# Spreading decay exponents by DMA instead of rebuilding them with small matmuls, in a gated delta-rule layer stack

## The reference, cut to what matters

```python
q, k, v = (silu(causal_conv(x @ W.T)) ...)        # 16 heads, dk 64, dv 128
q, k = l2_norm(q), l2_norm(k)
alpha = exp(-exp(A_log) * softplus(x @ Wa.T + dt_bias))
beta = 2 * sigmoid(x @ Wb.T)
# per head and token:
S = a_t * (S - b_t * k_t (k_t S)) + k_t v_t
o_t = S^T q_t
out = rms_norm(o) @ Wo.T
```

## Time and profile before

| | |
|---|---|
| median of 3 runs | 1748.54 us (1748.18 to 1759.42) |
| the profiled execution | 1763.2 us, span 1761.4 us |
| mean granted PE clock | 0.943 |
| PE busy | 1635.7 us, 93% |
| DVE busy | 1209.7 us, 69% |
| ACT busy | 800.0 us, 45% |
| POOL busy | 494.5 us, 28% |
| loop over the 32 units | about 93 to 1040 us of the span |

### The profile page before, as it was taken

The page is one execution under the profiler, slowest core; times in us unless marked ns, Lnnn a source line. Parts: engine busy times, 40 slices in busy tenths (PEclk is TensorE's granted clock), DMA queues, the critical chain, the costliest instruction groups (busy, mean ns, idle before and its releaser), DMA issues.

```text
span 1761.4 us, 32553 instructions
## 1 busy us (share of the span) xinstructions
PE 1635.7 (93%) x12575; PEld 993.5 (56%) x12575; DVE 1209.7 (69%) x2261; ACT 800.0 (45%) x1403; POOL 494.5 (28%) x986
## 2 busy tenths in 40 slices
PE   5798999999999999999999998887999899899998
PEld 1124666666666756666766766434545455554555
DVE  5955887888897878886767675647556755754533
ACT  5745565675655666564554443232232233222221
POOL 1033636445454543645445360000000000000000
PEclk9886997999997999999999997898999999999999
DMA  3000000000000000000000140000000000000000
GB/s 110 1 13 12 10 17 9 10 17 10 17 9 9 18 10 17 9 18 9 18 15 12 41 152 1 1 1 1 1 1 1 7 1 1 7 1 1 7 1 7
DMA packets 61337, 26.39 MB, mean 15 GB/s; under 512 B 54000, under 2 KB 57904, under 8 KB 60800
## 3 DMA queue, kind: packets, MB, share of 16 engines
q1 hardware_dynamic: 61184, 24.32, 5.3%
HBM read 16.37 MB, written 7.34 MB: 13 GB/s over the span
## 4 chain that ended last, share of the span: by engine, by line
PE 73%; DVE 17%; ACT 6%; issue 4%; DMA 0%; SPq 0%; POOL 0%; DVEq 0%; ACTq 0%
PE bank L825 7%; PE bank L516 6%; PE bank L809 6%; PE bank L812 6%; PE bank L555 4%; PE bank L617 3%; PE bank L544 3%; PE bank L489 3%; PE bank L457 3%; PE bank L772 2%; PE bank L566 2%; PE bank L470 2%; PE bank L644 2%; DVE vc L1244 2%; PE bank L426 2%
## 5 line engine op out<-in xcount | busy, mean ns | idle before, releaser
L1323 DVE TENSOR_TENSOR AM<-bank,et 128x512 f32<-128x512 f32 x192 | 129.6, 687 | 152.5 <-PE bank L516 78.3
L1702 POOL TENSOR_TENSOR SU<-SU 128x28 f32<-128x28 f32 (+6 forms) x448 | 206.8, 462 | 35.2
L1706 POOL TENSOR_TENSOR SU<-SU 128x28 f32<-128x28 f32 (+6 forms) x448 | 203.4, 454 | 35.1
L1681 POOL TENSOR_TENSOR st<-st,nh 128x4 f32<-128x4 f32 x16 | 18.8, 1176 | 654.3 <-DVE st L1221 633.5
L1018 ACT ACTIVATE et<-bank 128x512 f32<-128x512 f32 x192 | 115.4, 601 | 189.7 <-PE bank L492 105.8
L1244 DVE SCALAR_TENSOR_TENSOR vc<-vy,conv,vc 128x512 f32<-128x512 f32 x192 | 146.4, 763 | 6.9 <-ACT vc L966 2.4
L825 PEld LDWEIGHTS bank<-WQ,AM 128*128 128x128 f32 x1024 | 129.1, 192 | 32.4 <-issue 25.0
L825 PE MATMUL bank<-WQ,AM 128*128 128x128 f32 x1024 | 138.0, 278 | 3.6 <-DVE X L1577 3.6
L809 PE MATMUL bank<-xnT,KQ 128*128 128x512 f32 x256 | 137.5, 620 | 0.0
L812 PE MATMUL bank<-xnT,KQ 128*128 128x512 f32 x256 | 133.5, 603 | 2.1 <-DVE AM L1567 2.1
L516 PE MATMUL bank<-KQ 64*128 64x256 f32 (+1 forms) x512 | 121.5, 577 | 7.7 <-DVE AM L1323 3.8
(11 more groups left out here) (223 smaller groups left out, 3441.4 us busy)
## 6 DMA issues: line engine op xcount, KB each, us to landing
scratch<-AM SPq DMA_DIRECT2D x128, 48.0 KB, 1.8
SM<-SM SPq DMA_DIRECT2D x288, 2.0 KB
SU<-scratch SPq DMA_DIRECT2D x128, 32.0 KB
WQ<-in_wqkv_dram SPq DMA_DIRECT2D x1, 2048.0 KB, 8.9
KQ<-in_wg_dram SPq DMA_DIRECT2D x4, 512.0 KB, 7.5
KQ<-in_wu_dram SPq DMA_DIRECT2D x4, 512.0 KB, 8.1
WQ<-in_wd_dram SPq DMA_DIRECT2D x1, 2048.0 KB, 15.5
WQ<-in_wo_dram SPq DMA_DIRECT2D x1, 1024.0 KB, 9.7
```

Source lines behind the costliest of these rows:

```text
L1323: e.tensor_tensor(dst, bank[(3, 1)[hh]][:, :].rearrange("p (k t) -> p k t", k=2), et[:, q % 2, :].rearrange("p (k t) -> p k t", k=2), ALU. ...
L1702: e.tensor_tensor(tmp[:, :, 0:k, 0:15 - k], sub[:, :, 0:k, k:k + 1].to_broadcast([128, 2, k, 15 - k]), sub[:, :, k:k + 1, k + 1:16].to_bro ...
L1706: e.tensor_tensor(sub[:, :, 0:k, k + 1:16], sub[:, :, 0:k, k + 1:16], tmp[:, :, 0:k, 0:15 - k], ALU.subtract).then_inc(s_su, 1)
```

## The change

The exponents are no longer rebuilt on PE. For each pair of sequences, two DMAs write the target parts of gn to a DRAM tensor, ahead. For each unit, six DMAs spread them from there over all 128 partitions into EX (one row of 512 numbers read for each partition; the last two in pieces of 128 numbers). POOL adds the causal mask in EX, in place, by six operations. The source part becomes a number per partition: four small PE transposes per pair put it into CS (`sources`), and ACT's exponential takes it as its bias, from EX; for i = 4, 5 in two halves of 256 columns, since the source block differs. The gram products go over banks 3, 1 and 2 in turn and wait for fewer `am`. The bf16 split is gone. `exp` 0 and 1 of the next unit stand late in ACT's step, ahead of `vtanh(2g)`. Some DVE calls stand in another order, and gB, gE, gD have other partitions.

```diff
-            def rows(n):
-                for k in range(3):
-                    for r in range(3):
-                        if k == 0:
-                            e.dma_start(CRt[r:r + 1, sl, :, :], spl[hs[0], r, :]).then_inc(s_rows[sl], 16)
-                        else:
...
+            def lengths(p):
+                e.wait_ge(s_gs, p + 1)
+                for k in range(2):
+                    e.dma_start(ahead[p, :, :, k, :], gn[32 * k + 32:32 * k + 48, :].rearrange("h (b t) -> h b t", b=2)).then_inc(s_row, 16)
+                e.wait_ge(s_row, 32 * p + 32)
+            def spread(n, i):
+                p, h = n // NG, GH * (n % NG) + i % 2
+                if n:
+                    e.wait_ge(s_exp, 6 * (n - 1) + i + 1)
+                if i < 4:
+                    e.dma_start(EX[:, i, :], ahead[p, h:h + 1, i // 2, :, :].rearrange("o k t -> o (k t)").to_broadcast([128, 512])).then_inc(s_ring[i // 4], 16)
+                else:
+                    e.dma_start(EX[:, i, :].rearrange("p (x t) -> p x t", x=4),
+                                ahead[p, h:h + 1, :, :, 128:256].rearrange("o b k t -> o (b k) t").to_broadcast([128, 4, 128])).then_inc(s_ring[i // 4], 16)
...
             for n in range(NN):
+                if n + 1 < NN:
+                    if (n + 1) % NG == 0: lengths((n + 1) // NG)
+                    for i in range(6):
+                        spread(n + 1, i)
                 blocks(n)
-                if 0 < n < NN - 1: rows(n + 1)
...
-            def decay(n, i, hh):
...
+            def sources(p):
+                b = bank[0 if p else 2]
+                e.wait_ge(s_gs, p + 1)
+                for k in range(4):
+                    ins = e.transpose(b[:, 16 * k:16 * k + 16], gn[0:16, 128 * k:128 * k + 128], ident[0:16, 0:16])
             def gram(n, i):
                 if n or i:
-                    e.wait_ge(s_am, 6 * n + 2 * i)
+                    e.wait_ge(s_am, 6 * n + (0, 1, 3)[i])
...
-                        k3 = bank[(3, 1)[hh]][:, o:o + w].rearrange("p (k t) -> p k t", k=2)
+                        k3 = gbank(2 * i + hh)[:, o:o + w].rearrange("p (k t) -> p k t", k=2)
...
@@ PE, step @@
-                if has_g: decay(g, 0, 0)
+                if has_g: gram(g, 0)
...
             def exp(n, i):
-                e.wait_ge(s_ge, q + 1)
+                e.wait_ge(s_mk, q + 1)
...
-                e.activation(et[:, q % 2, :], bank[2][:, :], ACT.Exp).then_inc(s_exp, 1)
+                if i < 4:
+                    b = i // 2
+                    e.activation(et[:, q % 2, :], EX[:, i, :], ACT.Exp, bias=CS[:, p, 2 * b, h:h + 1]).then_inc(s_exp, 1)
+                else:
+                    e.activation(et[:, q % 2, 0:256], EX[:, i, 0:256], ACT.Exp, bias=CS[:, p, 1, h:h + 1])
+                    e.activation(et[:, q % 2, 256:512], EX[:, i, 256:512], ACT.Exp, bias=CS[:, p, 3, h:h + 1]).then_inc(s_exp, 1)
...
@@ ACT, step @@
                 if has_p: kcopy(2 * s + 2)
+                if g + 1 < NN: exp(g + 1, 0)
+                if g + 1 < NN: exp(g + 1, 1)
                 more(s, 6)
                 if has_g: vtanh(2 * g)
...
@@ DVE, step @@
-                if has_k: kconv(2 * s)
                 if has_l: lengths2(p)
+                if has_k: kconv(2 * s, [0, 1])
                 if has_g: am(g, 0)
                 if has_g: am(g, 1)
                 if has_j: inv_p(j, 1)
+                if has_k: kconv(2 * s, [2])
...
@@ POOL @@
+            def masks(n):
+                em = emask[:, :].rearrange("p (k t) -> p k t", k=2)
+                for i in range(6):
+                    e.wait_ge(s_ring[i // 4], (64 if i < 4 else 32) * (n + 1))
+                    if i < 4:
+                        x = EX[:, i, :].rearrange("p (k t) -> p k t", k=2)[:, :, 0:128]
+                        e.tensor_tensor(x, x, em, ALU.add).then_inc(s_mk, 1)
+                    else:
+                        x = EX[:, i, :].rearrange("p (b k t) -> p b k t", b=2, k=2)
+                        e.tensor_tensor(x, x, em.unsqueeze(1).to_broadcast([128, 2, 2, 128]), ALU.add).then_inc(s_mk, 1)
...
                 if gap(s + 1, "norm") is not None:
                     norm(gap(s + 1, "norm"))
+                if g + 1 < NN: masks(g + 1)
                 if g < NN: substitute(g)
```

More of the change, by code:

```diff
@@ L149, in program @@
         s_gab, s_gd, s_ga, s_gn, s_gl, s_gs = (sem(f"s_g{n}") for n in ("ab", "d", "a", "n", "l", "s"))
-        s_ge, s_gk, s_exp, s_am = (sem(f"s_{n}") for n in ("ge", "gk", "exp", "am"))
+        s_cst, s_cs, s_mk, s_gk, s_exp, s_am = (sem(f"s_{n}") for n in ("cst", "cs", "mk", "gk", "exp", "am"))
         s_bi, s_su, s_tt, s_i0, s_iy, s_ix, s_ia, s_ip, s_ib, s_ic, s_in, s_id, s_yfd, s_yfo, s_yfc = (
@@ L197, in wbank, with gbank @@
             return bank[1 if hh and n < NN - 3 else 4]
+        def gbank(q):
+            return bank[(3, 1, 2)[q % 3]]
         def wide(b):
@@ L231, in program @@
                 GAP[NG * p + 22] = ("signed", p)
+        for p in range(1, NP):
+            GAP[NG * (p + 1)] = ("sources", p)
         GAP[NN + LAG - 1] = ("norm", ("at", 0))
+        assert len(GAP) == 4 * NP - 1
         def gap(s, kind):
@@ L411, in gap_wait @@
                     e.wait_ge(s_sgx, p + 1)
+                p = gap(s, "sources")
+                if p is not None:
+                    e.wait_ge(s_cs, p + 1)
             def kproj(t):
@@ L449, in vproj @@
                 if hh:
[L450 removed]
+                    e.wait_ge(s_am, 6 * n + 6)
                 else:
@@ L863, in _ @@
                 more(s, 1)
-                if has_g: gram(g, 0)
-                if has_g: decay(g, 0, 1)
                 if has_w: squares(w)
                 more(s, 2)
-                if has_g: decay(g, 1, 0)
                 if has_g: gram(g, 1)
-                if has_g: decay(g, 1, 1)
                 if gap(s, "gates") is not None: gates(s // NG)
@@ L873, in _ @@
                 if gap(s, "signed") is not None: signed_mm(gap(s, "signed"), bank[0], s_vV, 2 * g - 1)
+                if gap(s, "sources") is not None: sources(gap(s, "sources"))
                 if has_j: inv_b(j, 1)
@@ L876, in _ @@
                 more(s, 3)
-                if has_g: decay(g, 2, 0)
                 if has_g: gram(g, 2)
@@ L882, in _ @@
                 more(s, 4)
-                if has_g: decay(g, 2, 1)
                 if has_g: vproj(2 * g)
@@ L998, in lengths1, with sources @@
                 e.activation(gn, gn, ACT.Ln).then_inc(s_gl, 1)
[L1000 to L1009 removed]
+            def sources(p):
+                e.wait_ge(s_cst, p + 1)
+                e.activation(CS[:, p].rearrange("p k h -> p (k h)"), bank[0 if p else 2][:, 0:64], ACT.Copy).then_inc(s_cs, 1)
             def exp(n, i):
[L1012 to L1013 removed]
+                q, p, h = 6 * n + i, n // NG, GH * (n % NG) + i % 2
+                if n % NG == 0 and i == 0:
+                    e.wait_ge(s_cs, p + 1)
+                e.wait_ge(s_mk, q + 1)
                 if q >= 2:
@@ L1080, in _ @@
             e.activation(sgn[:, :], sgn[:, :], ACT.Sign).then_inc(s_sgn, 1)
-            e.wait_ge(s_zero, 4)
+            e.wait_ge(s_zero, 3)
+            sources(0)
+            exp(0, 0)
+            exp(0, 1)
             def split1(q, ch, i):
@@ L1145, in _ @@
                 has_p = LAG <= s < NN - 1
-                has_l, p = s % NG == 0 and LAG < s <= NN, s // NG - 1
                 has_e = s % NG == NG - 1 and LAG < s < NN
-                if has_g: exp(g, 0)
                 if g == NN: vV(2 * g - 1)
-                if has_g: exp(g, 1)
-                if has_l: lengths2(p)
                 if has_k: ktanh(2 * s)
@@ L1157, in _ @@
                 if gap(s, "norm") is not None: norm(gap(s, "norm"))
-                if has_l: lengths3(p)
+                if gap(s, "sources") is not None: sources(gap(s, "sources"))
                 more(s, 2)
@@ L1653, in _ @@
                 more(s, 7)
-                if LAG < s < NN and s % NG > 2: gates2(s // NG, s % NG - 3)
+                if LAG < s < NN and s % NG in STEP_AT:
+                    for k in STEP_AT[s % NG]: gates2(s // NG, k)
                 if gap(s + 1, "norm") is not None: norm(gap(s + 1, "norm"))
@@ L1707, in substitute @@
                                     ALU.subtract).then_inc(s_su, 1)
+            def masks(n):
+                em = emask[:, :].rearrange("p (k t) -> p k t", k=2)
+                for i in range(6):
+                    e.wait_ge(s_ring[i // 4], (64 if i < 4 else 32) * (n + 1))
[5 more added lines that the diff above has]
+                        e.tensor_tensor(x, x, em.unsqueeze(1).to_broadcast([128, 2, 2, 128]), ALU.add).then_inc(s_mk, 1)
             norm(("l0", 1))
+            masks(0)
             for s in range(LAG, NN + LAG + 3):
```

118 lines of the change are left out of this document (27 added, 91 removed).

## The result

The changed kernel takes 1793.07 us, the median of 4 runs (1779.80 to 1806.29), beside 1750.47 us of the kernel before on the same chip (1748.18 to 1759.42). The ratio is 1.0234, 95% interval 1.0127 to 1.0340: slower by 2.3%. I had forecast 1736 us. The profiled execution is the slowest of the four, with a span of 1804.5 us.

What follows compares the result with a forecast made beforehand. PE was taken to set the step, with DVE close behind. Terms 31 - 7 + 22 + 13 - 30 - 28 + 5 + 6 = 12 us gained, from 1748.5 to 1736 us, range 1700 to 1770.

Steps and rivals of the forecast that it cites:

- A plain step with the key stage: DVE becomes the longer engine, its gram waits go; 26.4 us per step, 1.8 less, 31 us over 17 steps.
- PE loses the decays: Six decays of 0.53 us leave PE, 3.2 us per step; its need falls to 25.0 us, 24.0 without key stage.
- The last am's wait, 1.5 us: DVE's wait before the last am stays and grows from 1.38 to about 1.5 us, as exp 5 becomes two halves.
- Late plain steps, 2.8 us each: Steps without the key stage lose PE's 3.2 us, gain a 0.4 us wait; 22 us over eight steps.
- POOL and the queue: Masks add 7.0 us per step to POOL, fitting its idle time; blocks wait 0 to 1.5 us, hidden by slack.
- Norm steps: In six steps ACT's exponentials wait for masks behind POOL's norm; 5 us each, 30 us, plus 28 us of clock.
- Clock falls: Standstills slow PE's clock: 7 us each at g = 11, 19, 27, 30; 7 us for plain steps' idle pieces.
- (c): Rival: PE's idle pieces in plain steps bring the clock down there too; 1770 us, chance 0.18.
- (b): Rival: norm steps cost little and the clock holds; 48 us gained, 1700 us, chance 0.25.
- (d): Rival: POOL becomes the bound through stretched masks, or the change doesn't free the step; 1753 us, chance 0.07.
- Start: Step 0 loses six decays at low clock and reaches its blocks earlier; 5 us gained, bounds 0 and 8.
- The list of what would show it: Signs in the later profile: 26 to 27 us plain steps if right; waits, clock falls or PE idle if wrong.

Runs made afterwards that it cites:

- x2: Changed kernel with the gram banks in the order 3, 2, 1 instead of 3, 1, 2; 1748.36 us, ratio 0.9995.
- x11: Kernel before the change with only gram(g, 0) moved to the head of the step, ahead of decay and inv_a; 1894.87 us, ratio 1.0773.
- x1: Changed kernel with inv_a(j, 1) put back ahead of gram(g, 0) on TensorE; 1788.49 us, ratio 1.024.
- x6: x4 without the mask additions on GpSimd, exponents scaled to stay finite, so causal mask and true decays are left out; 1697.97 us, ratio 0.9694.
- x4: Changed kernel with both gram banks in the order 3, 2, 1 and GpSimd's masks ahead of the norm; 1723.53 us, ratio 0.9864.
- x3: Changed kernel with GpSimd's masks of the next step put ahead of the norm; 1751.04 us, ratio 1.0013.
- x10: Changed kernel with seven idle products ahead of gram(g, 0), in TensorE's stand at the head; 1776.50 us, ratio 1.0139.
- x9: x4 with idle products where TensorE stands, in steps with the key stage only; 1702.85 us, ratio 0.9728.

## Why the prediction was wrong

**The step that failed** is in "A plain step with the key stage": "Its waits for gram products (1.19 us) go, because gram 0 stands first and the third bank loosens the others." Standing first doesn't let it start. It needs bank 1, which `out(j, 1)` and ACT's `ot(j, 1)` of the step before hold until 1.6 us into the step. The old order had covered this wait with the decay and inv_a, so no row of before showed it as idle time of PE. The 1.19 us of DVE was its one sign, and I read it as PE being late with other work. Shown by x2 (the wait taken away by another bank: 45 us), by x11 (the wait laid bare in the old kernel: 1.61 us, step 28.2 to 29.8) and by x1 (the old order, put back alone, changing nothing).

The sizes: I had 26.4 us for a plain step with the key stage and 24.4 for a late one; they take 28.7 and 26.4 at the full clock (28.68 in the stretch above, 26.4 in step 25). 2.3 us on 17 steps and 2.0 on 8 are 55 us (the steps are 18 and 7; the sum stays the same). The miss is 1793 - 1736 = 57, but that the two come so close is luck. Added up step by step over the two profiles:

| part | forecast | measured |
|---|---|---|
| 25 plain steps | 46 us shorter, and 6 in slow stretches | 24 us longer |
| six norm steps | 45 us longer | 25 us longer |
| first pick-up | 5 us earlier | 3.5 us earlier |

The plain steps missed by 70 us and more: 55 by the length of a step at the full clock, the rest by stretches at the low clock and by steps 9 and 17. These went from 31.56 to 34.85 us, with 2.2 us of PE's idle time ahead of `out`, and no experiment looks at them alone. The norm steps came out 20 us better than I had them. With the banks turned, plain steps take 27.0 to 28.3 and 24.9 at the full clock (x2), so there the forecast was still 0.5 us and more too low.

**PE loses the decays:** right. 25.32 us of PE in a plain step, 23.16 late, where I had 25.0 and 24.0.

**The last am's wait, 1.5 us:** right, 1.43. The halves of exp 5 take 508 + 492 ns, 1.0 us where I took 0.8.

**Late plain steps, 2.8 us each:** wrong for the same reason; 0.8 (27.2 to 26.4), and 2.3 in x2. Taking "DVE has room there" for enough overlooked that the head of the step is one chain, copy to gram to am, whatever the engines' room.

**POOL and the queue:** right in kind. The masks take 835 and 1413 ns for the 0.94 and 1.6 us of the working, so 6.2 us for 7.0 per step, and a spread lands in 3.3 us. The substitution starts 8.4 us after the start of the last `am` (median of the steps), 7.6 before: a delay of 0.8, within the 0 to 1.5 of the working. That the masks cost nothing was too low: VectorE's taps grew from 763 to 870 ns beside them, which I had priced for POOL but not for DVE, and x6 is 26 us under x4, 17 to 26 of them for the masks. The Trainium skill, page GPSIMD Engine Reference, section Specifications, has the shared interface, which x6's 761 ns bears out. I applied it to one side only.

**Norm steps:** right in mechanism, too large in size. The stands are 5.70 and 3.76 us for 6.1 and 4.7 in g = 11. With the clock I had 58 us for them, 45 net of the decays' gain; they came out 25 us longer, and taking the cause away gives back 42 (x3). The clock was the oversized term: 7 us each in g = 11, 19, 27 and 30, where the steps had means of 0.81 to 0.91 and were 5.1 to 7.5 us longer in all, the stand included.

**Clock falls:** they come outside norm steps too, which was rival (c)'s mark, and (c)'s 1770 was nearer than mine. x10 puts some 17 us on those that hang on the head stand. Rival (c) had no cause for TensorE's gaps but less work; the cause was the bank. (b) fell with the norm steps, and (d) too: of ACT's 40.5 us of waiting for masks 37.8 lie in the six norm steps (4.67 us in g = 5 and 13, 5.90 in 11 and 19, 8.31 in 27 and 30), the rest at the start, and none in a plain step.

**Start:** the first pick-up comes 3.5 us earlier (126.32 for 129.79), of the 5 forecast. The step behind it is 8.5 us shorter (29.97 for 38.46), which I had priced only in the 6 us for slow stretches.

The list of what would show it had the right line at its end: PE idle for more than 2 us in plain steps at full clock, "a chain that I haven't seen is the bound". PE idled 3.36.

What stays open: which stands still bring the low clock in x4 and x9, and why the same stand brings it in one step and not in the next (1.61 us ahead of L505 stood at 200.70 in step 3 of the changed kernel, whose clock was 1.00, and again at 229.43 in step 4 at 0.75).

## What to carry to other kernels

Before moving an operation to the head of a step, list everything that it waits for, its output bank above all, and look up when the last reader of that bank ends. A wait that other work covers has no row in the trace; it appears when that work is removed or moved. In this kernel a stand of 1.6 us on the busiest engine cost more than its length (x11), so compare a stand's price at both clock levels before accepting it. When an engine gets new operations, price what they do to the neighbour as well, and look at what stands in front of them in its queue: swapping two calls on GpSimd gave 42 us here.
